# Order of the top-64 attention loop, place of one pair's statistics, and engine of one rounding, in a fused four-layer kernel

## What is computed

```
# layer 1, feed-forward: ternary weights, activations rounded to 8 bits per token
Wq = clip(round(W / w_scale), -1, 1) * w_scale
xq = clip(round(x * (127 / x_scale)), -128, 127) * (x_scale / 127)   # x_scale = max|x| of the token
h  = gelu(bitlinear(x, W1, b1)); out = bitlinear(h, W2, b2)          # h has 1024 columns
# layer 2, attention: 16 heads, only the 64 largest of 77 scores take part
scores = q @ k.T / sqrt(16)
vals, idx = top_k(scores, 64); scores = full(-big).at[idx].set(vals)
ctx = softmax(scores) @ v
```

## Time and profile before

| what | value |
|---|---|
| median of three executions | 897.32 us |
| profiled execution, its own time | 897.16 us |
| its span, first to last instruction | 895.4 us |
| TensorE busy | 801.0 us (89%) |
| VectorE busy | 655.2 us (73%) |
| ScalarE busy | 497.2 us (56%) |
| GpSimd busy | 531.4 us (59%) |
| mean granted TensorE clock | 0.968 of full speed |

### The profile page before, as it was taken

The page is one execution under the profiler, slowest core; times in us unless marked ns, Lnnn a source line. Parts: engine busy times, 40 slices in busy tenths (PEclk is TensorE's granted clock), DMA queues, the critical chain, the costliest instruction groups (busy, mean ns, idle before and its releaser), DMA issues.

```text
span 895.4 us, 18961 instructions
## 1 busy us (share of the span) xinstructions
PE 801.0 (89%) x5858; PEld 628.7 (70%) x5858; DVE 655.2 (73%) x2739; ACT 497.2 (56%) x1287; POOL 531.4 (59%) x721
## 2 busy tenths in 40 slices
PE   6999998998788676867887989999999999998897
PEld 5677775886566444645666779788778879987775
DVE  4888686888979999999999873455455542516887
ACT  5778764568997797978877331222112122226673
POOL 3565644676752978878775125456455545237883
PEclk9999999999999697979999899999999999999999
DMA  9200001000000082000222621222222243140011
GB/s 296 62 1 2 2 1 48 1 1 1 1 1 1 2 328 97 1 25 2 71 72 87 227 72 36 37 42 43 37 42 43 36 87 58 19 107 1 13 36 48
DMA packets 37823, 46.70 MB, mean 52 GB/s; under 512 B 4327, under 2 KB 33871, under 8 KB 37724
## 3 DMA queue, kind: packets, MB, share of 16 engines
q1 hardware_dynamic: 29243, 35.77, 11.9%
q0 software_dynamic: 8480, 9.72, 7.1%
HBM read 33.80 MB, written 11.68 MB: 51 GB/s over the span
## 4 chain that ended last, share of the span: by engine, by line
PE 64%; DVE 14%; ACT 8%; issue 6%; POOL 6%; another core or an unknown queue 1%; DMA 1%; DVEq 0%; ACTq 0%; POOLq 0%; SPq 0%
PE ps L3012 10%; PE ps L3023 10%; PE ps L2358 4%; PE ps L2454 3%; PE ps L2481 3%; PE ps L2780 3%; PE ps L2800 3%; PE ps L3067 2%; PE ps L3041 2%; PE ps L2439 2%; ACT ptall L1254 2%; PE ps L2466 2%; DVE experts L1812 1%; PE ps L2811 1%; PE ps L2866 1%
## 5 line engine op out<-in xcount | busy, mean ns | idle before, releaser
L2080 DVE COPY ptall<-experts 128x512 f32 x136 | 53.3, 434 | 97.8 <-PE ps L3012 49.1
L1388 ACT ACTIVATE wk<-ps 128x1024 f32<-128x1024 f32 x34 | 34.9, 1025 | 131.3 <-PE ps L3012 69.1
L3012 PE MATMUL ps<-xnT,ptall 128*128 128x128 f32 x896 | 105.0, 275 | 2.3 <-DVE ptall L2080 1.8
L3012 PEld LDWEIGHTS ps<-xnT,ptall 128*128 128x128 f32 x896 | 102.4, 192 | 3.0 <-issue 3.0
L3023 PE MATMUL ps<-experts,wk 128*128 x448 | 102.0, 381 | 1.4 <-ACT xkeep L1398 1.4
L3023 PEld LDWEIGHTS ps<-experts,wk 128*128 128x128 f32 x448 | 82.9, 190 | 17.0 <-issue 6.8
L848 POOL DMA_INDIRECT xn<-expert_in,rown x34 | 36.0, 1058 | 80.7 <-PE ps L2998 57.1
L646 POOL TENSOR_TENSOR experts<-experts,rden 128x616 f32<-128x616 f32 x32 | 38.9, 1217 | 46.8 <-DVE rden L1572 46.8
L872 POOL DMA_INDIRECT token_sum<-xkeep,dest x28 | 47.6, 1699 | 31.1 <-ACT xkeep L1398 22.5
L1229 ACT ACTIVATE experts<-experts 128x77 f32<-128x77 f32 x248 | 62.1, 258 | 0.0
L2358 PE MATMUL ps<-ones 128*128 128x256 bf16 x434 | 55.7, 286 | 5.8 <-POOL mone L599 5.8
(11 more groups left out here) (382 smaller groups left out, 2358.5 us busy)
## 6 DMA issues: line engine op xcount, KB each, us to landing
experts<-in_ew SPq DMA_DIRECT2D x16, 1024.0 KB, 8.5
xkeep<-in_bw SPq DMA_DIRECT2D x2, 1024.0 KB, 7.3
expert_in<-xkeep SPq DMA_DIRECT2D x8, 256.0 KB, 3.9
x<-token_sum SPq DMA_DIRECT2D x8, 256.0 KB, 3.8
out<-x SPq DMA_DIRECT2D x7, 256.0 KB, 2.2
x<-in_x SPq DMA_DIRECT2D x1, 1536.0 KB, 9.1
token_sum<-x SPq DMA_DIRECT2D x4, 256.0 KB, 2.6
token_sum<-x SPq DMA_DIRECT2D x1, 1024.0 KB, 4.5
```

What stands on the lines that cost most here:

```text
L2080: ins = nc.vector.tensor_copy(tilew[:, v, c, :], experts[:, bass.ds(e * EW + (c * FF + v * 512), 512)])
L3012: ins = nc.tensor.matmul(ps[j % 2][:, v, k * P:(k + 1) * P], tilew[:, v, c, k * P:(k + 1) * P], xTb[j % 3][:, c, :], start=c == 0, stop=c ...
```

## The change

Six edits, in the order of the diff:

1. GpSimd's `mid_hidden(b, 1)` rounds the second tile itself (a `tensor_scalar` of 128x1024), and ScalarE's `mid_magic(b, 1)` goes away; the first tile's rounding stays on ScalarE.
2. ScalarE's `top_out(k-3)` moves behind the exponentials for `k` below 32.
3. ScalarE's `top_turned_probs` comes one `k` later (item `k-3`), and stands right behind `top_scores(k+1)`, for `k` from 3 to 31; from 31 on the old place takes over.
4. VectorE's `top_stats(1)` moves from the top-64 loop to the last two steps but one of the middle stage, one half at `k = 16`, the other at `k = 17`.
5. TensorE's `top_values` comes one `k` later and right behind `top_scores(k+2)`; `top_turn` and `top_queries` of the next pair come one step later (`j = 4`, then 5 and 6) and stand ahead of `top_probs`.
6. The 14 warming matmuls fall away where a `top_final` stands in the same step (items 24 to 27).

```diff
--- before.py
+++ after.py
@@ -681,6 +681,13 @@
                 nc.gpsimd.tensor_scalar(big, big, EPS_Q, wstat[:, 5:6], ALU.max, ALU.mult)
                 gp.wait_ge(own_p.sem, n)
                 nc.gpsimd.tensor_tensor(fac, fac, mone[:, 0:1], ALU.pow).then_inc(ghs, 1)
+                if t:
+                    gp.wait_ge(ghs, TB * b + t + 1)
+                    gp.wait_ge(ghq, TB * b + t)
+                    if b:
+                        gp.wait_ge(ght, TB * b + t - 1)
+                    nc.gpsimd.tensor_scalar(hmag[t], hbuf[b % 2][t], fac, MAGIC, ALU.mult, ALU.add
+                                            ).then_inc(ghq, 1)
 
             gp.wait_ge(pv_p[0].sem, pv_p[0].past(SC))
             for h in range(2):
@@ -1283,10 +1290,8 @@
                         mid_norm_f(k)
                     if 0 <= k - 6 < B:
                         mid_norm_g(k - 6)
-                    if 0 <= k - 11 < B:
-                        if k == B + 10:
-                            top_queries(0, 1)
-                        mid_magic(k - 11, 1)
+                    if k == B + 10:
+                        top_queries(0, 1)
                     if k == B + 11:
                         top_scores(1)
                         mid_hidden_t(B - 1, 1)
@@ -1317,12 +1322,14 @@
                     if 1 <= k < N4 + 1:
                         top_abs(k - 1)
                     q, j = (k - 1) // ITEMS + 1, (k - 1) % ITEMS
-                    if k >= 3 and (k - 3) // 2 % 2:
+                    if k >= N4 and (k - 3) // 2 % 2:
                         top_out(k - 3)
                     if k == N4 + 1:
                         l5_norm_tile(B // 2, 0)
                     if 1 <= k < N4 - 1:
                         top_scores(k + 1)
+                    if 3 <= k < N4:
+                        top_turned_probs(k - 3)
                     if 1 <= k < N4:
                         top_exp(k - 1, 0)
                     if k == N4:
@@ -1339,9 +1346,11 @@
                     if k == 1:
                         for c in range(CH):
                             keys2(1, c)
+                    if 3 <= k < N4 and (k - 3) // 2 % 2:
+                        top_out(k - 3)
                     if k in top_parts:
                         top_residual(top_parts[k] // 4, top_parts[k] % 4, k)
-                    if 2 <= k < N4 + 2:
+                    if N4 - 1 <= k < N4 + 2:
                         top_turned_probs(k - 2)
                     if k - 1 in l5_at:
                         l5_norm(l5_at[k - 1])
@@ -1959,12 +1968,12 @@
                         mid_sum_g(k - 12, 0)
                     if k in (13, 14):
                         top_stats(0, [k - 13])
+                    if k in (B + 8, B + 9):
+                        top_stats(1, [k - B - 8])
                 drop_least(0)
                 for k in range(N4 + 2):
                     if 1 <= k < N4:
                         drop_least(k)
-                    if k == 1:
-                        top_stats(1)
                     if k == N4:
                         end_shift(N4 - 1)
                         end_norm(N4 - 2)
@@ -2785,15 +2794,15 @@
                     ins.then_inc(sc_p[4].sem, 1)
 
                 def top_probs(i):
-                    q, j = (i + 1) // ITEMS + 1, (i + 1) % ITEMS
+                    q, j = (i + 2) // ITEMS + 1, (i + 2) % ITEMS
                     pe.wait_ge(pt_s[4].sem, pt_s[4].past(i))
-                    if N4 - 9 <= i < N4 - 1:
+                    if N4 - 9 <= i < N4 - 1 and i + 2 not in top_parts:
                         warm(14, 4)
                     pe.wait_ge(nm_s, i + 1)
-                    if q < PAIRS and j == 3:
+                    if q < PAIRS and j == 4:
                         pe.wait_ge(xts[4].sem, xts[4].past(2 * q + 2))
-                    elif q < PAIRS and j in (4, 5):
-                        pe.wait_ge(q_s[4].sem, q_s[4].past(4 * q + 2 * (j - 3)))
+                    elif q < PAIRS and j in (5, 6):
+                        pe.wait_ge(q_s[4].sem, q_s[4].past(4 * q + 2 * (j - 4)))
                     for h in range(HG):
                         for t in range(TB):
                             at = (h % 2) * S + t * P
@@ -2804,6 +2813,8 @@
                 def top_values(i):
                     q, j, u = i // ITEMS, i % ITEMS, i % 2
                     s2 = j // 2 % 2
+                    if i - 1 in l5_at:
+                        pe.wait_ge(xts[5].sem, xts[5].past(l5_at[i - 1] + 1))
                     pe.wait_ge(pt_s[4].sem, pt_s[4].past(i + 1))
                     if s2 == 0 and i >= 4:
                         pe.wait_ge(oc_s, (i - 2) // 4 * 2 + u + 1)
@@ -2932,28 +2943,29 @@
                     if k == N4:
                         pe.wait_ge(sc_r[4].sem, sc_r[4].past(N4))
                         pe.wait_ge(done[4].sem, done[4].past(4 * (PAIRS - 1)))
+                    if 3 <= k < N4:
+                        top_values(k - 3)
                     if k in top_parts:
                         top_final(top_parts[k] // 4, top_parts[k] % 4, k)
+                    if q + 1 < PAIRS:
+                        if j == 4:
+                            top_turn(q + 1)
+                        if j in (5, 6):
+                            top_queries(q + 1, j - 5)
                     if 2 <= k < N4 + 2:
                         top_probs(k - 2)
                         if k - 2 in l5_at:
                             l5_flip_half(l5_at[k - 2], k)
-                        if k - 3 in l5_at:
-                            pe.wait_ge(xts[5].sem, xts[5].past(l5_at[k - 3] + 1))
                         if k == N4:
                             l5_logits_half(B // 2 - 1)
                             warm(6, 2)
                         if k == N4 + 1:
                             top_final(PAIRS - 1, 0, k)
-                        top_values(k - 2)
+                        if k >= N4 - 1:
+                            top_values(k - 2)
                         if k == N4 + 1:
                             top_final(PAIRS - 1, 1, k)
                             l5_flip(B // 2)
-                    if q + 1 < PAIRS:
-                        if j == 3:
-                            top_turn(q + 1)
-                        if j in (4, 5):
-                            top_queries(q + 1, j - 4)
                     if k >= N4 + 2:
                         if k == N4 + 2:
                             for m in range(2, 4):
```

## The result

The changed kernel takes 903.00 us (median of 20 executions, 899.16 to 906.05), the kernel before 900.83 us (median of 20, 895.31 to 903.31; the first three of them are the times shown above). The ratio is 1.0031 with the interval [1.0015, 1.0046]: slower by some 2.8 us. The forecast was 892.0 us, the range 888.0 to 897.5. It was built on the 897.32 us of three executions; 20 put the kernel before 3.5 us higher.

A forecast was written before the change was run, and what follows sets the result against it. VectorE was taken to bound the top-64 stage (TensorE's chain the late middle stage). 2.8 + 1.5 + 1.0 = 5.3 us off 897.16 gave 891.9, median 0.16 higher: 892.0 us, range 888.0 to 897.5.

The forecast's parts named there:

- Turned probabilities one step later: Top-64 stage, edits 2, 3, 5: scores get 3.8 us of slack, so all 3.8 us of VectorE's gaps go.
- What is late next: Top-64 stage: queries ahead of `top_probs` delay steps around k = 14 and 22; 1.0 us lost, ends 0 and 3.8.
- the walk: Top-64 timing from E (item's end on VectorE): k = 13 ends 2.25 us, k = 14 5.0, after next E.
- Edit 6: cost or gain nothing: Top-64 stage: the 4 x 14 warming matmuls stand beside VectorE's work; removal changes nothing unless the clock falls.
- The tail stays; I take 0: After the top-64 stage's last item the new order meets the old at k = 31: 0 us, bounds -1 and +1.
- Statistics 1.5 us: Second pair's statistics free 1.59 us of VectorE in the top-64 stage and cost 0.1 in the middle stage; net 1.5.
- middle stage 1.0: Second tile's rounding on GpSimd, taken at 1.28 us each, relieves ScalarE; net 1.0 us won, bounds 0 and 4.
- B: Rival, chance 0.20: top-64 lateness at k = 14 and 22 is 0.7 us or more higher, gaps move; 894.8 us.
- E: Rival, chance 0.09: TensorE's clock stays at 1.2 GHz around the top-64 queries, scores come 3.3 us late; 903.5 us.
- C: Rival, chance 0.12: ScalarE is the middle stage's real limit, which gives 4.2 us instead of 1.0; 888.8 us.
- D: Rival, chance 0.09: middle-stage GpSimd roundings of 2.55 us delay the next tile, 2.4 us lost; 895.3 us.
- A: The forecast itself for the whole kernel, chance 0.50: 892.0 us, its own range 889.5 to 894.

The follow-up runs named there:

- hybrid: Changed kernel with items 8q+1 to 8q+3 and the next pair's turn and queries held at their old steps; ratio to the kernel before 0.9945.
- mid_warm: Kernel before with edits 1 and 4, and without the warming matmuls of items 24 to 27, old order otherwise; ratio to the kernel before 0.9950.
- order_only: Changed kernel with edits 1 and 4 undone, so the top-64 reordering and the removed warming alone; ratio to the kernel before 1.0032.
- warm_back: Changed kernel with the 14 warming matmuls of items 24 to 27 put back (edit 6 undone); ratio to the kernel before 1.0064.
- mid_only: Kernel before with edits 1 and 4 alone, top-64 order as before; ratio to the kernel before 0.9974.
- hybrid_tail: Like hybrid, with items 27 and 28 also in the old order; median 893.11 us, ratio to the kernel before 0.9925.
- gap_warm: Changed kernel with 20 small warming matmuls, never read, ahead of each item's scores from item 5 on; ratio to the kernel before 0.9988.
- edit1: Kernel before with edit 1 alone (second tile rounded by GpSimd); ratio to the kernel before 0.9981.

## Why the prediction was wrong

- **Turned probabilities one step later, "all 3.8 us of gaps would go": right in mechanism, but the gain was booked on the wrong edit.** Of the old gaps those at 12 and 31 went, ScalarE's wait fell from 23.8 to 0.7 us (with 6.4 us of waiting for transposes come up ahead of the absolute values), and hybrid, the order without the moved queries, has 0.8 us of gaps left. But mid_warm, in the old order, has only 1.3, and its ratio is 0.9950 against hybrid's 0.9945. What the new order adds to edit 6 is some 0.5 us, and less than the intervals can tell.
- **"What is late next ... I charge 0.5 us at each of the two places, 1.0 in all; the ends are 0 and 3.8": this step failed.** Measured were 11.7 us of gaps in the profiled execution, 6.8 in order_only, 8.0 in warm_back; even the upper end was too low. The places were named right in part (15, 16, 23, 24 forecast; 7, 8, 16, 20, 23, 24 found), the size was not. The waits for the queries at k = 13 and 14, 1.6 and 3.0 us by the walk, came true (1.66 and 3.00). What failed is where the steps begin. The walk let k = 13 begin on time, at E + 1.25. ScalarE began it 1.7 us late, at 363.94 us, where item 12 ended at 361.0; at k = 12 it had been 1.8 late (357.73 after 354.7), at k = 11 3.1 (352.65 after 348.3). The trace of the kernel before had it too: there the same absolute values start at 363.79 us, 3.4 behind item 12's end at 360.4, where the walk put 1.25. So k = 15 began at 380.78, 5.8 us late where the walk had 3.75, and its scores, with no slack left, made the gap of 2.22 us. At k = 21 TensorE was at half clock besides, and k = 22 inherited it. The walk also left out that `top_probs` waits for the copies of the queries, and `top_abs` of the next step for its transposes (6.4 us in the kernel after). And "pair 1 has no final there" was taken for no cost: items 7 and 8 wait 1.6 us. The ends of a cost have to come from rows, but 3.8 was "all gaps come back", the size of what is won, not a bound of the new wait.
- **"Edit 6: cost or gain nothing": wrong in size.** The warming matmuls stand ahead of the transposes on the chain: 14 take 1.5 us at full clock and 3.17 us at the lower level, and their removal gave 2.2 us (mid_warm) to 3 us (warm_back). The forecast had itself read them ahead of the longest gap and then costed them beside VectorE's work.
- **"The tail stays; I take 0": not for the order as it is.** TensorE waits 4.21 us for the turned probabilities, the clock is 0.50 from 486 to 492 us, and all behind it is late; the 14 warming matmuls, 1.53 us in the forecast, take 3.17:

```profile
487.05 1.08 PE L2822 MATMUL ps<-ptall,experts 77*32 77x256 f32 x8 [4.21 <-ACT ptall L1261]
488.06 3.17 PE L2367 MATMUL ps<-ones 128*128 128x256 bf16 x14
491.03 1.73 PE L2809 MATMUL ps<-ident,experts 128*77 128x128 f32 x8
```

  That part took 18.6 us against 16.4. Not all of it is the order: mid_only, whose order is the old one, had 18.0. hybrid_tail's 15.7 is some 3 us less than hybrid's, order and clock together.
- **Statistics 1.5 us and middle stage 1.0: right in their sum.** mid_only gives 2.3 of the 2.5 us. Of the two, edit 1 alone gave 1.7 us and edit 4 alone 0.4 by their ratios, with intervals of 2 us each way, so how the 2.3 us split stays open. GpSimd's operation took 1.12 us, under my 1.28. The Trainium skill (GPSIMD Engine Reference, section 3) gave an estimate of 0.9 to 1.6 us, and the trace agrees.
- **The rivals.** What came is B's mechanism, the queries ahead of the transposes, at several times its price, with a part of E's clock: gap_warm won 3.9 us. B had assumed that the new gaps couldn't exceed the old. C and D did not happen. E's 903.5 us lies near the 903.0 measured by luck: E said 6.2 us more than before and 2.8 came, from a base that lies 3.5 us higher. The same shift is in the forecast's own miss: of the 11.0 us between 892.0 and 903.0 it is 3.5, and the change is 7.5. A's lower end, 889.5, does not follow from its terms either: 3.8, 1.5 and the statistics' 1.5 make 6.8 us, so 890.5.

By the ratios, at 0.9 us for each thousandth: middle stage and statistics -2.3 (mid_only), edit 6 -2.2 (mid_warm), the new order of the other items -0.5 (hybrid), turn and queries one step later, with the three items of each pair that stand with them, +7.7 (from hybrid to the kernel after). These are steps of one chain of ratios from 1 to 1.0031, so they add up to the whole by their making; that they do confirms nothing. The last one contains the lower clock, of which gap_warm gave back 3.9 us. Each step is the difference of two ratios with an interval of some 2 us each way, so only the last is far outside its error.

## What to carry to other kernels

When work is moved one step later in a software pipeline, ask not only whether its own consumer still gets it in time, but what round trip (made on one engine, copied by another, awaited by the first) now has to fit within a single step, and walk at least two steps on, at the lower clock level too. Judge matmuls that keep an engine warm by what is queued behind them. And a bound for a new wait is the length of its own chain, never the amount that the change hopes to win.

## What was unexpected of the hardware

- One kernel's executions differ by up to 8 us (895.31 to 903.31 for the kernel before, 899.16 to 906.05 after), while hybrid_tail's six lie within 1.6 and edit1's twelve within 5.1. Stretches of 0.50 clock sit at other places in other traces; that an order with slack spreads less because it hides them is my reading, not shown, and mid_only speaks against it: its order is the old one, and its twelve lie within 2.5 us.
- GpSimd's 128x1024 `TENSOR_SCALAR` with one input took 1.12 us, less than its 128x512 addition of two inputs, 1.28.
- 20 small matmuls ahead of every item's scores from item 5 on, 190 more in the 50 us from 400 on, went with shorter gaps on VectorE (4.9 us for 11.7) and lifted the clock from 0.79 to 1.00; 14 ahead of the transposes of four items cost 2 to 3 us. Where they stand is what differs most.
